# A graph network kernel: the moments of its dense rows are spread anew over two stages, and a seam of its last stage gets other work

## What is computed

```python
edge_index = jnp.stack([src, dst])
x = _layernorm(x + _L0_gnn_ref(x, ...))   # attention over the edges, per target
x = _layernorm(x + _L1_gnn_ref(x, ...))   # messages with a mean per target, a matrix, a second layernorm
x = _layernorm(x + _L2_gnn_ref(x, ...))   # products of source rows with edge features, summed per target
x = _layernorm(x + _L3_gnn_ref(x, ...))   # hypergraph convolution twice, batch norm between
```

## Time and profile before

| | |
|---|---|
| Median of three runs | 2510.71 us (2508.42 to 2510.8) |
| The profiled execution | 2507.46 us, of which the span of instructions is 2505.7 |
| Busy: POOL, DVE, PE, ACT | 71%, 63%, 56%, 34% of the span |
| Stages in the trace | attention 266 to 682 us, messages 690 to 1083, tail from 1401 to the end |

### The profile page before, as it was taken

One profiled execution on the slowest core, in us unless ns is written; L12 is line 12 of the kernel. 1 busy time (PEld: TensorE's weight loads), 2 busy tenths in 40 slices (PEclk: granted clock), 3 DMA queues, 4 the chain that ended last, 5 costly groups with the idle time before them and its releaser, 6 DMA issues. The chain is left out here.

```text
span 2505.7 us, 21855 instructions
## 1 busy us (share of the span) xinstructions
PE 1393.9 (56%) x4580; PEld 725.9 (29%) x4580; DVE 1579.2 (63%) x4917; ACT 861.4 (34%) x1813; POOL 1776.4 (71%) x1419
## 2 busy tenths in 40 slices
PE   6778488888546666547888366354555640011121
PEld 1444244444313333213433244122223330001110
DVE  8889378878727989949899454243444464534443
ACT  0111156667515767735877211011112320000000
POOL 5774677777078888148787587788757878777887
PEclk8899699999768887768999687677777865555555
DMA  1111244444254566344666577567796863323331
GB/s 25 25 33 41 76 110 123 123 123 113 57 113 115 142 162 152 100 99 105 145 147 137 121 203 200 138 171 194 158 228 163 245 181 81 86 63 72 72 72 43
DMA packets 358128, 297.94 MB, mean 119 GB/s; under 512 B 110941, under 2 KB 312428, under 8 KB 357981
## 3 DMA queue, kind: packets, MB, share of 16 engines
q1 hardware_dynamic: 260397, 225.43, 33.4%
q0 software_dynamic: 97600, 71.11, 14.7%
HBM read 199.75 MB, written 96.70 MB: 118 GB/s over the span
## 5 line engine op out<-in xcount | busy, mean ns | idle before, releaser
L2219 DVE TENSOR_TENSOR_SCAN tl_S<-tl_same,tl_S,tl_pX 128x500 f32<-128x500 bf16 x96 | 120.3, 1253 | 317.6 <-issue 219.1
L2108 PE MATMUL tl_pX<-k_ident,tl_ga 125*128 125x125 f32 x400 | 84.6, 349 | 421.1 <-DMA tl_ga<-table_TE,k_s_idxE 321.8
L481 POOL DMA_INDIRECT tl_ga<-table_TE,k_s_idxE x200 | 243.0, 1215 | 63.4 <-issue 58.5
L2108 PEld LDWEIGHTS tl_pX<-k_ident,tl_ga 125*128 125x128 f32 x400 | 57.6, 178 | 437.0 <-DMA tl_ga<-table_TE,k_s_idxE 331.4
L481 POOL DMA_INDIRECT ms_ga<-table_T,k_idxS x100 | 143.4, 1434 | 36.1 <-issue 29.6
L481 POOL DMA_INDIRECT tl_ga<-table_TH,k_send x100 | 123.1, 1231 | 51.7 <-issue 51.1
L1288 PE MATMUL tl_pCon<-dr_BC,dn_cT 128*128 128x512 f32 x196 | 130.6, 754 | 51.2 <-DVE dr_o L1307 21.6
L283 POOL DMA_INDIRECT table_ptab<-k_ef,ix_scatI x100 | 124.8, 1248 | 47.9 <-issue 47.9
L481 POOL DMA_INDIRECT at_ga<-x,k_src x100 | 126.5, 1265 | 44.7 <-issue 27.3
L481 POOL DMA_INDIRECT at_gb<-xw,at_dstI x100 | 128.9, 1289 | 35.5 <-issue 29.0
L481 POOL DMA_INDIRECT eq_ga<-table_T,k_idxS x100 | 126.1, 1261 | 35.0 <-issue 30.0
(11 more groups left out here) (469 smaller groups left out, 4363.9 us busy)
## 6 DMA issues: line engine op xcount, KB each, us to landing
dr_x<-x SPq DMA_DIRECT2D x97, 256.0 KB
result<-dr_o SPq DMA_DIRECT2D x97, 256.0 KB
dm_xT<-xT SPq DMA_DIRECT2D x32, 768.0 KB
tl_fac<-table_dinv SPq DMA_DIRECT2D x50, 250.0 KB
table_T<-at_y SPq DMA_DIRECT2D x50, 224.0 KB
table_T<-ms_y SPq DMA_DIRECT2D x50, 224.0 KB
table_T<-eq_y SPq DMA_DIRECT2D x50, 224.0 KB
table_TE<-tl_y SPq DMA_DIRECT2D x50, 224.0 KB
```

What stands on the lines that cost most here:

```text
L481: nc.gpsimd.indirect_dma_start(out=buf[:, k, :], out_offset=None, in_=table, in_offset=bass.IndirectOffsetOnAxis(ap=index[:, CT * c + k:CT ...
L2108: last = nc.tensor.transpose(pX[j % 2][:, k * TP:(k + 1) * TP], ga[j % RG][:, k, :], K["ident"][0:TP, 0:TP])
L2219: nc.vector.tensor_tensor_scan(S[i][:], same[j % RM][:], pX[i][:, 0:CE], 0.0 if j % NC == 0 else S[1 - i][:, CE - 1:CE], ALU.mult, ALU.add ...
```

## The change

Three things change.

1. **The moments' schedule.** Attention now does three supers instead of five, spread over 24 turns: mostly one group a turn (`AT_QUADS` gives the first group of each of eight turns: two groups in turns 0 and 6, one in turns 1 to 5, and the transposes in turn 7). Loads and squares of a part stand two and one turn ahead of turns 0, 2 and 5 of the eight. Messages do the other eight supers: three groups in each of turns 0 to 23, so a part is loaded and squared every turn.
2. **Two PSUM banks in messages.** `dn.pS` is a list of two there, used in turn by `bank_of`. The transposes of a full super and the first matmuls of the next one now stand in the same turn of TensorE, and the matmuls wait for the `s_kept` of the super before the last one.
3. **The tail's seam.** Of the state gathers 32 instead of 16 stand behind the last gather from TE. `dense_turn` gives turns 25 to 37 two dense groups as before, turns 38 to 49 one instead of two, and the 12 groups so left (63 to 74) are done at the seam (`dense_seam`) by SP, TensorE, ACT and VectorE, behind the last J_NODE chunk and the batch norm, ahead of the first J_EDGE chunk.

```diff
+AT_SUPERS = 3
+AT_QUADS = (0, 2, 3, 4, 5, 6, 7, 9, 9)
+AT_PARTS = (0, 2, 5)
-MA = 20
@@ attention, TensorE (ACT, DVE and SP follow)
-                    if s < MA:
-                        dn.moments(pe, s)
+                    if s < 8 * AT_SUPERS:
+                        dn.moments(pe, s // 8, range(AT_QUADS[s % 8], AT_QUADS[s % 8 + 1]))
+                        if s % 8 == 7:
+                            dn.turn_moments(pe, s // 8)
@@ messages
-        dn.pS = a.ps("pS", [128, 512])
+        dn.pS = [a.ps(f"pS{i}", [128, 512]) for i in range(2)]
...
-                    dn.load_turned(sp, MA + s + 2)
+                    dn.load_turned(sp, dn.ms_part(s + 2))
...
-                    dn.moments(pe, MA + s)
+                    if s > 0 and s % 3 == 0:
+                        dn.turn_moments(pe, AT_SUPERS + s // 3 - 1)
+                    if dn.ms_part(s) is not None:
+                        dn.moments(pe, AT_SUPERS + s // 3, range(3 * (s % 3), 3 * (s % 3) + 3))
@@ in moments, of a super h
-        if j % 4 == 0:
-            need(pe, self.s_kept, h)
+            if k == 0:
+                need(pe, self.s_kept, h + 1 - len(self.pS))
@@ tail
+SEAM, WIDE_SEAM, SEAM_ROWS = 4, 8, 12
+KEPT = 2 * NC - SEAM - WIDE_SEAM
+
 def dense_turn(t):
-    first = [min(DQ, u if u < NC else min(2 * u - NC, u + NC)) for u in (t, t + 1)]
-    return range(first[0], first[1])
+    def first(u):
+        if u <= NC:
+            return u
+        if u <= KEPT:
+            return 2 * u - NC
+        return min(DQ, u + KEPT - NC + (SEAM_ROWS if u > 2 * NC else 0))
+
+    return range(first(t) + (SEAM_ROWS if t == 2 * NC else 0), first(t + 1))
+
+def dense_seam():
+    n = dense_turn(2 * NC).start
+    return range(n - SEAM_ROWS, n)
@@ SP; the other engines have the same loop with expand, turned and combine
+                if t == J_EDGE:
+                    for d in dense_seam():
+                        dn.load_rows(sp, d + 2)
+                        dn.store_rows(sp, d)
@@ POOL
-                if c + SEAM < NC - SEAM:
+                if c + SEAM < NC - WIDE_SEAM:
                     keep_states(c + SEAM)
-            for c in range(NC - SEAM, NC):
+            for c in range(NC - WIDE_SEAM, NC):
                 keep_states(c)
```

More of the change, by code:

```diff
@@ L1067, in bases, with at_part, ms_part, bank_of @@
         last.then_inc(s_base, 1)
-    def stage(self, j):
-        return 3 * (j // 4) + j % 4 if j < MT and j % 4 < 3 else None
+    def at_part(self, s):
+        r = s % 8
+        return 3 * (s // 8) + AT_PARTS.index(r) if 0 <= s < 8 * AT_SUPERS and r in AT_PARTS else None
+    def ms_part(self, s):
+        return 3 * AT_SUPERS + s if 0 <= s < 3 * (SUPERS - AT_SUPERS) else None
+    def bank_of(self, h):
+        return self.pS[h % len(self.pS)]
     def span(self, n):
         return 512 * 3 * n, min(512 * 3 * n + 512 * 3, 128 * DT)
-    def load_turned(self, sp, j):
-        n = self.stage(j)
+    def load_turned(self, sp, n):
         if n is None:
@@ L1083, in load_turned, with squares @@
         sp.dma_start(self.xT[:, n % 2, 0:b - a], self.g["xT"][:, a:b]).then_inc(self.s_xT[n % 2], 16)
-    def squares(self, act, j):
-        n = self.stage(j)
+    def squares(self, act, n):
         if n is None:
@@ L1121, in flatten, with moments @@
[L1121 to L1125, removed]
+    def moments(self, pe, h, quads):
+        nc, pS = self.nc, self.bank_of(h)
+        count = min(PACK, DQ - PACK * h)
+        for k in quads:
+            if k >= count:
+                return
+            n = 3 * h + k // 3
+            a, b = self.span(n)
+            u = 512 * (k % 3)
+            w = min(512, b - a - u)
+            if k % 3 == 0:
+                pe.wait_ge(self.s_xT[n % 2], 16 * (n // 2 + 1))
+                pe.wait_ge(self.s_z2, n + 1)
+            if k == 0:
+                need(pe, self.s_kept, h + 1 - len(self.pS))
+            at = PW - NV - NV * k
+            nc.tensor.matmul(pS[0:PW, 0:w], self.Vx[:, at:at + PW], self.xT[:, n % 2, u:u + w], start=k == 0, stop=False)
+            last = nc.tensor.matmul(pS[0:PW, 0:w], self.Vz[:, at:at + PW], self.z2[:, n % 2, u:u + w], start=False, stop=k == count - 1)
+            if k % 3 == 2 or k == count - 1:
+                last.then_inc(self.s_mom, 1)
@@ L1126, in flatten, with turn_moments @@
+    def turn_moments(self, pe, h):
+        pe.wait_ge(self.s_flat, h + 1)
+        for i in range(4):
+            last = self.nc.tensor.transpose(self.bank_of(h)[:, i * PW:(i + 1) * PW], self.flat[:, i * 128:(i + 1) * 128], self.K["ident"][0:PW, 0:PW])
+        last.then_inc(self.s_mT, 1)
+    def flatten(self, act, h):
         act.wait_ge(self.s_mom, 3 * h + 3)
         need(act, self.s_mT, h)
-        self.nc.scalar.activation(self.flat[:], self.pS[0:PW, :], ACT.Identity, bias=self.off[:]).then_inc(self.s_flat, 1)
@@ L1521, in _ @@
                     message(s + 1)
[L1522 removed]
+                    dn.squares(act, dn.ms_part(s + 1))
                 if live(s - 1):
@@ L2145, in _ @@
                     rows(job(t - 1))
+                if t == J_EDGE:
+                    for d in dense_seam():
+                        dn.expand(pe, d)
                 if job(t) is not None:
```

61 lines of the change are left out of this document (20 added, 41 removed).

## The result

| | before | after |
|---|---|---|
| Median | 2509.57 us (2507.94 to 2510.80, 4 runs) | 2468.22 us (2465.79 to 2471.30, 4 runs) |
| Ratio | | 0.9836, 95% interval 0.9819 to 0.9853 |
| Span of the profiled execution | 2505.7 | 2465.8 |

What follows compares the result with a forecast made beforehand. Bounds: TensorE and VectorE's ring in attention, POOL just under; POOL's gathers in messages' first half; POOL's 21.5 us seam wait. -21 + 7 - 19 = -33 from 2507.46 gave 2474.5, with half the 3.25 to the median 2477; range 2463 to 2494.

Steps and rivals of the forecast that it cites:

- Attention, -21 forecast: Attention: one group a turn fills TensorE's wait for `o`, turns stay at 12.80 us; saves 21, ends -24 and -11.
- Rival A: Attention: TensorE's clock falls as moments are taken out; attention saves only 11, total 2487 us; chance 0.15.
- Messages, +7 forecast: Messages: with a square in every turn, the stage costs 7 us more, ends 0 and +14.
- if all turns are like this: Messages, second half: every turn with a square takes 13.27 us against a mean of 12.79, costing 5.8 us.
- The loop through store and load: Messages: a part's load queues behind `store`, which waits for ACT's y, and ACT's square waits for that load.
- rival C: Messages: with a part every turn, loads land later and no turn recovers; 30 us slower, about 2540; chance 0.05.
- The seam, -19 forecast: Tail: 16 more state gathers behind the last TE gather remove POOL's 21.5 us wait; saves 19, ends -21 and -6.
- The price among the TE gathers: Tail before the seam: twelve chunks of TE gathers in a row, not eight, cost POOL 2 us.
- The lag: Seam: 45.4 us from the end of the last TE gather to the gather that waits for TH, taken as unchanged.
- The late landing of the gathers: Tail: TE gathers land behind their issue, 6.7 us a chunk against 6.05, lagging by 8 us over twelve chunks.
- rival D: Whole kernel: all goes at its best, -24 + 0 - 21 = -45, 2463 us; chance 0.13.
- best end: The most favourable end forecast for each part: attention -24, messages 0, seam -21 us.

Runs made afterwards that it cites:

- the bunched run: The changed kernel with attention's three supers done three groups a turn in turns 0 to 11 and no moments afterwards: 2474.69 us (ratio 0.9859).
- the run where it was held: The changed kernel with 32 state gathers at the seam, but turns 38 to 49 doing two dense groups again and none at the seam: 2485.6 us (0.9889).

## Why the prediction came out as it did

- **Attention, -21 forecast, -23.1 measured.** Right in its mechanism: one group fills the wait for `o` (12.6 us against 12.8), eight turns take 106.8 us where the sum had 106.9, and up to the last gather POOL's waits are all that there is to win. That gather came 21.3 us earlier, as forecast. The other 2 lie behind it: the last two turns had gone at the lower clock before, 13.96 and 13.88 us, and are 13.53 and 12.28 now. That the groups of the third super kept the clock up there is likely; two us are less than the stage scatters by. Rival A did not come, and the bunched run shows what it rested on.
- **Messages, +7 forecast, +1.2 measured.** The same messages take 394.4 to 399.8 us in six traces against 395.8 before, so the cost is somewhere between nothing and 4 us, and 7 was too much. The step that failed is "if all turns are like this". The turn of 13.27 us was a turn of VectorE, 13.10 from scan to scan, with a kept bank's copy in it; ACT only followed. A turn with a square and without the copy is 12.55. The loop through store and load that I named for rival C exists (14.6 us for 16.8 of squares) but is in most turns no longer than VectorE's, so the forecast added what was already hidden. I should have set the wait's length beside VectorE's idle time, which was nearly none: 146.8 of 153.5 us busy there.
- **The seam, -19 forecast, -20.4 measured.** Right: the whole wait goes. The price among the TE gathers, put at 2 us, was nothing: POOL waits for a buffer three times there, 0.3 us each, its usual distance. The lag was assumed unchanged; to the last store it was 39.9 and is 33.9 to 39.0. The late landing of the gathers, from which the price was worked out, is not what held POOL in the run where it was held; late dense loads were, of which the earlier trace rows had shown one. I cost the dense groups' move as a thing that has to be ready in time; it is the part that makes the seam work: without it the kernel is 17 us slower (2485.6 against 2468.8).
- **Two banks, nothing forecast.** With one bank TensorE waits 16.3 us, and neither the stage nor the total shows a cost beyond its scatter.
- **The sum.** -33 against -39.9 in the profiled spans: 2.1 from attention, 5.8 from messages, 1.4 from the seam make 9.3; 2.6 went the other way in stages that were not changed. The rest of the 8.8 us between 2477 and 2468.2 is the step from the profiled execution to the median, put at 2.5 and measured 0.6. The errors of the three parts have one sign, so they did not cancel: each part came within 1.2 us of its best end (-24, 0, -21). The result lies nearer to rival D (2463, chance 0.13) than to the forecast, and at the edge of the forecast's own range. The mechanisms of attention and the seam were right, the sizes too cautious.

## What to carry to other kernels

A wait on one engine is worth what the next engine leaves idle: before a new cost is put on it, its turn has to be laid beside the turn of the engine that is busy throughout. Filler for a seam has two sides: what is put in it, and what is taken out ahead of it; here the second decided. And work that is spread so thinly that it just fills each turn's wait kept the clock up here, and was cheaper than the same work in lumps by a few us.

## What was unexpected of the hardware

TensorE's clock fell and rose within one turn of 13.5 us: the matmul behind a wait of 1.76 us took 2.03 us, one of like shape 4.4 us later 1.00, in three turns one after the other and with 62.3 us busy of 80. With one group in each turn the same matmul took 1.10, and the granted clock of the stretch was 0.99 instead of 0.86.
